# Second attention of a one-core Trainium2 kernel: selection products of 48 rows in pairs, one buffer of transposed keys, key splits and value copies on POOL

## What is computed

```python
qkv = x @ w_attn                      # x: (8, 512, 128) after layernorm
q = qkv[..., :128]                    # 16 heads of 8
k, v = qkv[..., 128:136], qkv[..., 136:144]
att = einsum('bhqd,bkd->bhqk', q, k) / sqrt(8)    # causal
y = softmax(att) @ v
x = x + y @ w_proj
```

## Time and profile before

| what | value |
|---|---|
| median of 3 runs | 853.83 us (848.96 to 860.17) |
| the profiled execution | 861.02 us, span 859.3 us |
| PE busy | 681.4 us (79%) |
| DVE busy | 583.3 us (68%) |
| ACT busy | 349.4 us (41%) |
| POOL busy | 328.8 us (38%) |
| mean granted PE clock | 0.906 of full speed |

### The profile page before, as it was taken

One profiled execution on the slowest core, in us unless ns is written; L12 is line 12 of the kernel. 1 busy time (PEld: TensorE's weight loads), 2 busy tenths in 40 slices (PEclk: granted clock), 3 DMA queues, 4 the chain that ended last, 5 costly groups with the idle time before them and its releaser, 6 DMA issues. The chain is left out here.

```text
span 859.3 us, 14978 instructions
## 1 busy us (share of the span) xinstructions
PE 681.4 (79%) x4376; PEld 413.4 (48%) x4409; DVE 583.3 (68%) x1923; ACT 349.4 (41%) x748; POOL 328.8 (38%) x430
## 2 busy tenths in 40 slices
PE   1579989984048999999974779898989898898794
PEld 1445666652025788777762224444444444443353
DVE  8378888886921312544357988888889898977373
ACT  0322333304302212222311127666666666666761
POOL 0256656640065636677630003333333332333330
PEclk9999999997558859999995579999999999999996
DMA  9200000000411212222234213020404040300021
GB/s 297 80 1 1 0 1 0 1 1 26 134 40 32 37 19 35 34 40 38 35 77 55 37 22 49 12 57 3 56 4 56 3 57 9 50 4 3 1 62 38
DMA packets 40350, 32.44 MB, mean 38 GB/s; under 512 B 3608, under 2 KB 36936, under 8 KB 40280
## 3 DMA queue, kind: packets, MB, share of 16 engines
q1 hardware_dynamic: 30448, 23.51, 12.6%
q0 software_dynamic: 7840, 6.86, 5.4%
q10 hardware_dynamic: 1992, 1.21, 0.8%
HBM read 13.60 MB, written 8.13 MB: 25 GB/s over the span
## 5 line engine op out<-in xcount | busy, mean ns | idle before, releaser
L1602 ACT ACTIVATE pexp<-wide 128x512 f32<-128x512 f32 (+2 forms) x384 | 183.7, 543 | 118.5 <-PE wide L1791 112.3
L1551 POOL TENSOR_SCALAR_AFFINE_SELECT pexp<-pexp 128x256 f32<-128x256 f32 x256 | 107.3, 422 | 284.1 <-ACT pexp L1602 282.6
L1414 DVE CUSTOM_DVE_ANT_0 masked<-bank,mask_qk 128x384 f32<-128x384 f32 (+3 forms) x356 | 155.2, 480 | 22.0 <-PE bank L1742 20.0
L1791 PE MATMUL wide<-qT,kTe 128*128 128x256 bf16 (+3 forms) x501 | 120.7, 301 | 19.0 <-ACT pexp L1602 8.8
L1070 ACT ACTIVATE hT<-wide,b1T 128x512 f32<-128x512 f32 x64 | 43.5, 687 | 162.8 <-PE wide L1090 134.3
L1742 PE MATMUL bank<-kTm,qT 128*128 128x384 bf16 (+3 forms) x348 | 89.0, 320 | 17.1 <-DVE mx L1414 8.7
L1804 PE MATMUL bank<-pexp,vx 128*32 128x512 f32 (+3 forms) x1024 | 95.5, 445 | 0.8 <-POOL pexp L1551 0.8
L945 POOL DMA_INDIRECT x_dram<-yg,row_u x40 | 63.9, 1596 | 58.0 <-DVE yg L994 49.5
L1414 DVE CUSTOM_DVE_ANT_0 masked<-wide,mask_qk 128x256 f32<-128x256 f32 (+3 forms) x156 | 74.3, 499 | 15.5 <-PE wide L1742 12.9
L938 POOL DMA_INDIRECT x_row<-xln_dram,row_u x64 | 61.8, 965 | 52.8 <-DVE slot_tok L815 33.6
L1099 PE MATMUL bank<-w_sb,hT 128*128 128x128 f32 x512 | 75.4, 292 | 3.2 <-issue 3.2
(11 more groups left out here) (232 smaller groups left out, 1071.8 us busy)
## 6 DMA issues: line engine op xcount, KB each, us to landing
qT<-qp SPq DMA_DIRECT2D x135, 64.0 KB
x_sb<-in_L_attn_x SPq DMA_DIRECT2D x8, 256.0 KB, 6.7
w_sb<-in_L_ffn_w SPq DMA_DIRECT2D x1, 2048.0 KB, 13.1
xln_dram<-rx SPq DMA_DIRECT2D x8, 256.0 KB, 2.3
out_x<-x_sb SPq DMA_DIRECT2D x8, 256.0 KB, 2.3
x_dram<-x_sb SPq DMA_DIRECT2D x5, 256.0 KB, 3.5
x_sb<-x_dram SPq DMA_DIRECT2D x5, 256.0 KB, 3.0
x_row<-xln_dram,row_u POOLq DMA_INDIRECT x64
```

What stands on the lines that cost most here:

```text
L1414: ins = nc.vector.tensor_tensor_reduce(out=masked[:, n % 4, at], in0=bank_of(n)[:, at], in1=mask_qk[:, T - w:T], scale=1.0, scalar=LEAST, ...
L1551: nc.gpsimd.affine_select(out=pexp[:, n % 4, :, 0:P], in_=pexp[:, n % 4, :, 0:P], pattern=[[0, 2], [1, P]], compare_op=ALU.is_ge, fill=0.0 ...
L1602: nc.scalar.activation(pexp[:, (2 * step + h // 2) % 4, h % 2:h % 2 + nh, 0:w], psE[m % 3][:, 0:nh * w].rearrange("p (h t) -> p h t", h=nh ...
L1791: ins = nc.tensor.matmul(psE[m % 3][:, hh * w:(hh + 1) * w], kTe[:, par, j * P:(j + 1) * P], qT[:, b % QB, 4 * qd + h + hh, j * P:T], star ...
```

## The change

Each half of the heads has its own contraction blocks. The blocks for the six largest of the nine part products (q0k0, q1k0, q2k0, q0k1, q1k1, q0k2) stand in rows 0 to 47 for heads 0 to 7 and in rows 64 to 111 for heads 8 to 15; blocks 6, 7 and 14 hold the remaining three and are shared. The selection product uses those 48 rows only, so it finds the maximum of a slightly coarser score, and two such products, of head h and head h+8, are issued one behind the other into two banks, at row tiles 0 and 64. Units are listed in such pairs and placed in pairs (`PAIRS_IN_STEP`). The scores use 123 rows of the same buffer `kTm`, which now holds three sequences and the constant rows; `kTe` and its copy are gone. The key splits, the slot copies (four now) and the copy into `vx` are POOL's, whose loop is written out with them (`pool_turn`). A pair waits for the rows of both halves of the heads. The core of the diff:

```diff
@@ -58,7 +58,11 @@
...
-    QR = PARTS * PARTS * L
+    BLOCKS = 2 * P // 16 - 1
+    QR = BLOCKS * L
+    LARGE = 6 * L
+    ROWS_OF_HALF = (((0, 3, 5), (1, 4, 6), (2, 7, 14)), ((8, 11, 13), (9, 12, 6), (10, 7, 14)))
+    KEYS_IN_BLOCKS = ((0, 0, 2, 0, 3), (1, 0, 2, 3, 5), (1, 0, 1, 7, 8), (2, 0, 2, 5, 7))
@@ -119,7 +123,7 @@
...
-        kTm = sb("kTm", [P, 2, T], BF16)
+        kTm = sb("kTm", [P, QB, T], BF16)
@@ -1201,10 +1205,11 @@
...
-        for h0 in range(0, HEADS, 4):
+        for h0 in range(0, HEADS // 2, 4):
...
-                max_units += [(k, h, nh) for h in range(h0, h0 + 4, nh)]
+                for h in range(h0, h0 + 4, nh):
+                    max_units += [(k, h, nh), (k, h + HEADS // 2, nh)]
@@ -1263,8 +1267,8 @@
...
-        IN_STEP = (4, 3, 2, 2, 1, 2, 2, 2, 5, 4, 3, 3, 2, 4, 2, 3)
-        AHEAD = sum(IN_STEP[SHIFT_STEP:])
+        PAIRS_IN_STEP = (2, 2, 1, 1, 1, 1, 1, 0, 2, 2, 2, 1, 1, 1, 2, 2)
+        AHEAD = 2 * sum(PAIRS_IN_STEP[SHIFT_STEP:])
@@ -1357,46 +1361,45 @@
...
-            return ops(kx3[:, :, :, n, :], kp[:, n].unsqueeze(2).broadcast_to([P, NT, PARTS, L]))
...
+            part, g0, ng, lo, hi = KEYS_IN_BLOCKS[n]
+            return ops(kx3[:, :, g0:g0 + ng, lo % 8:lo % 8 + hi - lo, :],
+                       kp[:, part].unsqueeze(2).unsqueeze(2).broadcast_to([P, NT, ng, hi - lo, L]))
...
-        def dve_k_parts(dve, b, ops=range(5)):
...
-            dve.wait_ge(q_kx.sem, q_kx.at(b, 0))
-            split(dve, q_kpart, b, kv2[:, :, 0:L], k_rest[:, :, :], [kp[:, n] for n in range(PARTS)], ops)
...
-        def dve_k_slots(dve, b):
...
-                fill_k_slots(nc.vector.tensor_copy, n).then_inc(q_kx.sem, 1)
...
+            split(pool, nc.gpsimd, q_qpart, b, psA[:, :], q_rest[:, :], [qp[:, n] for n in range(PARTS)], ops)
...
+        def pool_k_parts(pool, b):
+            pool.wait_ge(q_kv.sem, q_kv.at(b, 1))
+            pool.wait_ge(q_kx.sem, q_kx.at(b, 0))
+            split(pool, nc.gpsimd, q_kpart, b, kv2[:, :, 0:L], k_rest[:, :, :], [kp[:, n] for n in range(PARTS)])
...
+        def pool_k_slots(pool, b):
+            pool.wait_ge(q_kpart.sem, q_kpart.at(b, 5))
+            pool.wait_ge(q_kTp.sem, q_kTp.at(b, 0))
...
+                fill_k_slots(nc.gpsimd.tensor_copy, n).then_inc(q_kx.sem, 1)
...
+        def pool_v(pool, b, par):
+            pool.wait_ge(q_kv.sem, q_kv.at(b, 1))
...
-            nc.vector.tensor_copy(vx[:, par, :, 0:L], kv2[:, :, L:2 * L]).then_inc(q_v.sem, 1)
...
-        def dve_kTe(dve, b, par):
...
-            nc.vector.tensor_copy(kTe[0:QR, par, :], kTm[0:QR, par, :]).then_inc(q_kTe.sem, 1)
+                pool.wait_ge(q_av.sem, q_av.at(b - 1, 0))
+            nc.gpsimd.tensor_copy(vx[:, par, :, 0:L], kv2[:, :, L:2 * L]).then_inc(q_v.sem, 1)
@@ -1463,17 +1466,10 @@
...
-                        dve_kTe(dve, b + 1, 1 - b % 2)
-                        dve_v(dve, b + 1, 1 - b % 2)
...
-                        dve_k_parts(dve, b + 2, {"A": (0,), "B": (1,), "C": (2, 3), "D": (4,)}[place])
...
-                    dve_k_slots(dve, b + 2)
@@ -1552,10 +1541,26 @@
...
+        def pool_turn(pool, b, middle=True, front=True):
+            for s in range(STEPS):
+                if middle and s == V_STEP:
+                    pool_v(pool, b + 1, 1 - b % 2)
+                if front and s == K_SPLIT_STEP:
+                    pool_k_parts(pool, b + 2)
+                if front and s == SLOT_STEP:
+                    pool_k_slots(pool, b + 2)
+                pool_causal(pool, b, 2 * s)
+                pool_causal(pool, b, 2 * s + 1)
+
...
-            with nc.gpsimd.Fori(0, B) as b:
-                for n in range(NX):
-                    pool_causal(pool, b, n)
+            pool_k_parts(pool, 0)
+            pool_k_slots(pool, 0)
+            pool.wait_ge(q_init.sem, q_init.total(4))
+            pool_v(pool, 0, 0)
+            pool_k_parts(pool, 1)
+            pool_k_slots(pool, 1)
+            for b in range(B):
+                pool_turn(pool, b, middle=b + 1 < B, front=b + 2 < B)
@@ -1584,11 +1589,11 @@
...
-            nc.scalar.activation(kTm[0:QR, par, :], psA[:, :].bitcast(BF16)[0:QR, 0:T], ACT.Copy).then_inc(q_kTm.sem, 1)
+            if b >= QB:
+                act.wait_ge(q_sp.sem, q_sp.at(b - QB, NS))
+            nc.scalar.activation(kTm[0:QR, b % QB, :], psA[:, :].bitcast(BF16)[0:QR, 0:T], ACT.Copy).then_inc(q_kTm.sem, 1)
@@ -1678,8 +1683,8 @@
...
-                for j in range(PARTS):
-                    row = (n * PARTS + j) * L
+                for block in ROWS_OF_HALF[half][n]:
+                    row = block * L
@@ -1726,22 +1731,28 @@
...
-            pe.wait_ge(q_kx.sem, q_kx.at(b, PARTS))
+            pe.wait_ge(q_kx.sem, q_kx.at(b, len(KEYS_IN_BLOCKS)))
...
-                                          kx3[:, k].rearrange("p n j l -> p (n j l)"), ident_bf[:, :])
+                                          kx3[:, k].rearrange("p g n l -> p (g n l)")[:, 0:QR], ident_bf[:, :])
...
-        def pe_max_unit(pe, b, n, place):
+        def pe_max_pair(pe, b, n, places):
+
...
-            pe.wait_ge(q_row[h // 8].sem, q_row[h // 8].at(b, PARTS * PARTS))
+            for half in range(2):
+                pe.wait_ge(q_row[half].sem, q_row[half].at(b, PARTS * PARTS))
...
-                ins = nc.tensor.matmul(place[:, hh * w:(hh + 1) * w], qT[:, b % QB, h + hh, k * P:(k + 1) * P],
-                                       kTm[:, b % 2, 0:w], start=True, stop=True)
-            ins.then_inc(q_smp.sem, 1)
+                for half, place in enumerate(places):
+                    rows = slice(64 * half, 64 * half + LARGE)
+                    ins = nc.tensor.matmul(place[:, hh * w:(hh + 1) * w],
+                                           qT[rows, b % QB, 8 * half + h + hh, k * P:(k + 1) * P],
+                                           kTm[rows, b % QB, 0:w], start=True, stop=True)
+                    if hh == nh - 1:
+                        ins.then_inc(q_smp.sem, 1)
@@ -1757,13 +1768,14 @@
...
-                pe_max_unit(pe, b, n, bank[i])
+                if n % 2:
+                    pe_max_pair(pe, b, n - 1, (bank[unit_bank[n - 1]], bank[i]))
...
-                pe_max_unit(pe, 0, n, psM4[n % len(psM4)])
...
+                pe_max_pair(pe, 0, n, (psM4[n % len(psM4)], psM4[n % len(psM4) + 1]))
@@ -1778,18 +1790,16 @@
...
-                pe.wait_ge(q_kTe.sem, q_kTe.at(b, 1))
...
-                    ins = nc.tensor.matmul(psE[m % 3][:, hh * w:(hh + 1) * w], kTe[:, par, j * P:(j + 1) * P],
-                                           qT[:, b % QB, 4 * qd + h + hh, j * P:T], start=True, stop=True)
+                    ins = nc.tensor.matmul(psE[m % 3][:, hh * w:(hh + 1) * w], kTm[0:QR + PARTS, b % QB, j * P:(j + 1) * P],
+                                           qT[0:QR + PARTS, b % QB, 4 * qd + h + hh, j * P:T], start=True, stop=True)
@@ -1937,8 +1947,8 @@
...
-            nc.vector.memset(kTm[64:P, :, :], 0.0).then_inc(s_zero.sem, 1)
-            nc.vector.memset(qT[64:P, :, :, :], 0.0).then_inc(s_zero.sem, 1)
+            nc.vector.memset(qT[64:P, :, 0:HEADS // 2, :], 0.0).then_inc(s_zero.sem, 1)
+            nc.vector.memset(qT[0:64, :, HEADS // 2:HEADS, :], 0.0).then_inc(s_zero.sem, 1)
@@ -1959,6 +1969,9 @@
...
+            pool.wait_ge(s_c.sem, s_c.total(16))
+            nc.gpsimd.tensor_copy(kTm[96:P, :, :], const("shift_rows")[96:P, :].unsqueeze(2).broadcast_to([P - 96, QB, T])).then_inc(s_zero.sem, 1)
+            pool.wait_ge(s_zero.sem, s_zero.total(3))
```

More of the change, by code:

```diff
@@ L1229, in build @@
         vx = scratch("vx", [P, 2, NT, 32])
[L1230 to L1231 removed]
+        kx3 = scratch("kx3", [P, NT, 2, 8, L], BF16)
         mx = scratch("mx", [P, NT, HEADS])
@@ L1367, in split @@
                 if n:
[L1368 removed]
+                    engine.wait_ge(sig.sem, sig.at(b, n))
                 if n % 2 == 0:
[L1370 removed]
+                    on.tensor_copy(part, whole if n == 0 else rest).then_inc(sig.sem, 1)
                 else:
[L1372 to L1377 removed]
@@ L1395, in dve_kTe, with dve_q_parts @@
-        def dve_kTe(dve, b, par):
-            dve.wait_ge(q_kTm.sem, q_kTm.at(b, 1))
-            if b:
-                dve.wait_ge(q_sp.sem, q_sp.at(b - 1, 0))
-            nc.vector.tensor_copy(kTe[0:QR, par, :], kTm[0:QR, par, :]).then_inc(q_kTe.sem, 1)
+                    on.tensor_tensor(rest, whole if n == 1 else rest, part, ALU.subtract).then_inc(sig.sem, 1)
+        def dve_q_parts(dve, b, ops):
+            split(dve, nc.vector, q_qpart, b, psA[:, :], q_rest[:, :], [qp[:, n] for n in range(PARTS)], ops)
@@ L1465, in dve_turn @@
                         dve_divide(dve, b - 1, tail_of(b).divide[s, place])
-                    if middle and s == KTE_STEP and place == "A":
-                        dve_kTe(dve, b + 1, 1 - b % 2)
-                        dve_v(dve, b + 1, 1 - b % 2)
                     if tail and (s, place) == tail_of(b).stats:
@@ L1986, in constants @@
```

(2 more changed lines are left out.)

64 lines of the change are left out of this document (20 added, 44 removed).

## The result

The changed kernel takes 876.15 us in the median of 4 runs (872.64 to 884.27), the kernel before 851.81; the ratio is 1.028, with an interval from 1.018 to 1.039. It is slower by some 24 us where the forecast, 861, had 7.5: inside the range, but the forecast loss is a third of the measured one. The profiled executions (884.27 and 861.02 us) have spans of 882.5 and 859.3 us.

A forecast was written before the change was run, and what follows sets the result against it. PE and DVE were taken to bound each other, POOL and ACT following. Turns at 42.5 us for six turns gave about +5.4, the start +2.1: +7.5 on 853.8 makes 861 us, range 840 to 880.

The forecast's parts named there:

- waits for y at four places: Sign of being right: PE waits 0.3 to 0.8 us for DVE's y in steps 1 to 4, one such wait before.
- one for POOL's masking in step 6: Sign of being right: step 6's values product waits for POOL, where none did before.
- PE's net near zero: Overlap of paired selection products against shape switches, per turn on PE: about 0, from -4.3 to +7.6 us.
- DVE's relief: Key splits, slot copies and copies to kTe and vx leave DVE: 2.2 of its 36.4 us per turn.
- PE's products: Paired selection products take 4.3 us per turn instead of 8.6; 37 switches at 0.11 cost 4.1.
- The divide behind the pair: Steps 1 to 4, place B: two units ahead of DVE's divide instead of one; +2.1 us per turn, from 0 to 3.0.
- POOL's new work: Step 6: both maskings queue behind POOL's key splits, delaying the values product; +0.9 us per turn, from 0 to 2.0.
- What takes it back: Vanished DVE waits give -1.0 us by step 8, fewer units in steps 8 to 11 -0.7; +0.9 remains per turn.
- The first and the seventh turn: First turn without divides, seventh without splits: each charged half the price of a full turn.
- The start: First pair needs both halves' rows, +4.1 us; key splits and slots drop from DVE, -2.0; net +2.1 once.
- Dear switches: Rival: pairs at B pay 0.20 us twice, or tiles do not overlap; turns +2.7, total 877 us; chance 0.24.
- The relief counts: Rival: switches cost 0.03, POOL's splits hide, PE and DVE get lighter; turn 39.2, total 842 us; chance 0.20.
- Nothing shows: Rival: slack of steps 12 to 15 absorbs late divides, DVE's backlog the start's 4.1; 854 us; chance 0.10.

The follow-up runs named there:

- e4: Changed kernel with each selection product over rows 0 to 119 instead of 48 rows, pairs kept at their places: 865.20 us, ratio 1.0333, full turns 44.07 to 44.20.
- e11: Single units at the old places, but selection products over 48 rows of their half instead of 120: 893.90 us in one run.
- e1: Changed kernel with DVE's divide ahead of the maxima of its place in steps 1 to 4: 853.49 us, ratio 1.0194.
- e6: Changed kernel with single selection units over 120 rows at the old places and numbers, POOL keeping splits and copies: 861.82 us, ratio 1.0154.
- e2: Changed kernel with POOL's key splits, slot copies and value copy behind the two maskings of their step: 858.42 us, ratio 1.0257.
- e7: Changed kernel with one pair moved from step 10 to step 7: 872.52 us, ratio 1.0222, full turns 43.09 to 43.25.
- e10: Changed kernel with single units over 120 rows at the old places, and POOL's splits and copies behind the maskings: 859.27 us, ratio 1.0082.
- e12: Changed kernel with divide first, POOL's maskings first, a pair in step 7, none in step 12, and the old single-unit start: 849.80 us, ratio 0.9992.
- e8: The changed kernel unaltered, measured once more: 875.40 us, ratio 1.0294, full turns 44.07 to 44.15.
- e3: Changed kernel with the turns' key splits and slot copies back on DVE at their old places: 858.22 us, ratio 1.0253.
- e9: Changed kernel with divide ahead of maxima, POOL's splits and copies behind maskings, and one pair in step 7: 866.70 us, ratio 1.0166.

## Why the prediction was right, and where it was wrong

**The direction and the range** were right, by the mechanisms that were named: waits for y at four places, one for POOL's masking in step 6, PE's net near zero, DVE's relief without worth (1.6 us, where 2.2 was forecast). The size was not: a turn of 44.1 is outside the 42 to 43 us that would have shown the forecast right, and 876 is inside the range because the range is wide.

**PE's products: right.** Pairs start together, a switch costs 0.11 and not 0.20, and e4 shows the sum: the same turn with and without row tiles. In detail the term was about 1 us too dear: without row tiles PE is busy 1.06 us more, where 4.3 less the switches had left next to nothing. Why is open, and it reached no turn. That changing tiling mode drains the engine (the Trainium skill, TensorEngine Tiling (Array Packing), Key Properties) agrees with e11, whose switches add 4.9 us of PE work; the page has no price, and the rows here have 0.11.

**The divide behind the pair: the size near, half of it from another cause.** Predicted lateness after steps 1 to 4 was 0.75, 1.31, 1.91, 2.06; measured at the values products of the steps behind them, 2 to 5, it is 1.18, 1.75, 1.77, 2.76. I let a wait for ACT swallow 0.5 of the fourth divide ("of which a wait for ACT inside that section takes 0.5: +0.15") and subtracted 0.4 for steps 5 to 7; PE's transposition of y waits 0.63 for that divide (616.26), and at step 5 the turn is 2.76 late, not 2.1. e1 gives 0.71 of that back, 1.27 of it all. The cause of the first 1.2 us is not the divide: they stay in e1 and fall to 0.38 in e6. They are not the switches either, since e4 has them too (1.18). So they belong to pairs at places where fewer and narrower single units stood.

**POOL's new work: right.** +0.9 predicted, +1.10 at step 6, 1.06 in the turn (e2), 1.11 (e6). The small casts take 0.21 us.

**"What takes it back" is the term that failed.** Steps 5 to 8 came out near the forecast: -0.4 and -1.0 were put down for them, and the lateness falls by 0.51 from step 6 to 7 and by 1.05 from 7 to 8. (Of the two waits that vanish there, the profile puts the one of 0.51 down to DVE; the one of 0.46 it puts down to no engine.) The second part, -0.7 in steps 8 to 11, rests on the words "PE, which then is the later of the two". It was DVE: with no pair in step 7 it stands idle for 2.24 and 1.28 us, starts its second half 24.03 us after step 0's values product where it started at 20.72, and works without a gap from there, so nothing is taken back (2.30 at step 8, 2.54 at step 13). I had counted the units of steps 8 to 11, fewer for DVE too, and not asked when DVE gets the first. e7 shows it from the other side: one pair moved into step 7, PE's lateness at step 8 unchanged, 0.9 us shorter. So a turn lost 2.46, not 0.9: 0.70 more by step 8 (2.30 for 1.6), and 0.86 more behind it (+0.16 for -0.7).

**The first and the seventh turn** were put at half the price of a full one, 0.45 each, and cost 4.5 and 3.7. In the seventh it is the divides (e1: 38.40), which stand at other places there and hold PE up for 1.20 and 1.56 us; I had priced only the full turn's. In the first, the stretch ahead of step 0's values product is 1.2 us longer, with the clock at 0.51 for 0.69 (the kernel before first):

```profile
503.63:513.40 9.77, 8.35 (x33) 3.46 (x32) 8.53 (x44) 3.30 (x7) 1.22 (x3) 0.69 0.02 6
505.28:516.26 10.98, 7.01 (x33) 1.79 (x31) 8.46 (x48) 2.95 (x7) 0.97 (x3) 0.51 0.02 4
```

Then 2.0 us are lost by step 2 (0.2 in e10, with single units) and 1.6 at step 6, where PE waits 1.50 us for POOL (none of it in e2): the pairs' places and POOL, as in a full turn but dearer. That the start in pairs causes it is not shown: e10 has that start and a first turn of 40.86 at a clock of 0.87, and e12, which has the old start, needs the same 11.1 us ahead of step 0's values product as e8. A first turn also repeats less well than a full one (44.26 and, in e8, 45.59 for the same kernel).

**The start:** +2.1 predicted, +4.15 measured; the forecast missed half of it. PE's first maxima wait 5.10 us for the rows:

```profile
472.55 0.61 PE L1751 MATMUL bank<-kTm,qT 48*128 48x128 bf16 x8 [5.10 <-DMA qT<-qp]
```

They begin 7.17 us after the product at 465.38, where they began 1.87 after it (467.88 to 469.75): 5.3 late, not 4.1. DVE's way from its first maximum to the copy of mT takes 31.99 us for 33.09, so 1.1 is given back, not 2.0. With the old start e12 is at 34.53.

**The rivals.** Dear switches came out nearest in time (877) and wrong in cause: its price of 0.20 is not there, and e4 excludes it. "The relief counts" is refuted for this place of the splits by e3 and e10; e9's one turn of 40.81, 0.8 under the kernel before, shows no cause of its own. "Nothing shows" would have needed a slack in the second half that DVE doesn't have.

The ledger of a full turn: 44.1, less 1.2 (divide), less 1.06 (POOL), less 0.9 (step 7), gives 40.9; e9's shortest turns are 40.81 and 41.42, and e12's 41.3, with its pair kept out of step 12. Over the whole program the full turns cost 12.4 us where 4.5 was forecast, the first and the seventh 8.2 for 0.9, the start 4.15 for 2.1.
